# Reordering the DMA queue and VectorE's program of a fused modulated-linear and per-token head-attention kernel

## What is computed

```
def modulated(x, s, aff_w, aff_b, w, b):          # one layer, per batch
    style = s @ aff_w.T + aff_b                   # 512 numbers
    demod = rsqrt(sum((w * style)**2, axis=in) + 1e-8)
    return (x * style) @ w.T * demod + b

x  = x + clip(modulated(x, cond, L0 ...), -256, 256)         # layer L0
kx = modulated(x, cond, K ...).reshape(tokens, 16 heads, 32)  # layer K; q = k = v = kx
A  = softmax(kx @ kx.T / sqrt(32))                # per token, 16 x 16 over its own heads
x  = x + modulated((A @ kx).reshape(tokens, 512), cond, O ...)   # layer O
```

## Time and profile before

| | us |
|---|---|
| three runs: median (lowest to highest) | 783.5 (782.16 to 788.72) |
| the profiled execution, its own time | 782.16 |
| its span, first to last instruction | 780.4 |
| what lies around the span | 1.8 |
| PE busy | 723.8 (93%) |
| PEld (weight loads) busy | 702.9 (90%) |
| VectorE busy | 553.3 (71%) |
| ScalarE busy | 510.1 (65%) |
| transfers of the one hardware queue, share of 16 DMA engines | 78.4% |

### The profile page before, as it was taken

One profiled execution on the slowest core, in us unless ns is written; L12 is line 12 of the kernel. 1 busy time (PEld: TensorE's weight loads), 2 busy tenths in 40 slices (PEclk: granted clock), 3 DMA queues, 4 the chain that ended last, 5 costly groups with the idle time before them and its releaser, 6 DMA issues.

```text
span 780.4 us, 21455 instructions
## 1 busy us (share of the span) xinstructions
PE 723.8 (93%) x8848; PEld 702.9 (90%) x8848; DVE 553.3 (71%) x1040; ACT 510.1 (65%) x1036; POOL 11.7 (1%) x8
## 2 busy tenths in 40 slices
PE   5999788999999999999999999999999999998676
PEld 4999678989999999999999999999999999997566
DVE  4555765778877777787787777778788777776562
ACT  4265547767776766777676677777677776675353
POOL 2300000000000000000000000000000000000000
PEclk9799898999999999999999999999999999998888
DMA  8028686898889988888878988888888889876763
GB/s 297 28 63 198 160 194 185 225 220 218 202 211 227 230 219 230 227 218 209 214 199 216 220 239 223 228 220 223 221 198 210 220 228 232 213 185 151 167 180 108
DMA packets 235778, 157.15 MB, mean 201 GB/s; under 512 B 143265, under 2 KB 225185, under 8 KB 235681
## 3 DMA queue, kind: packets, MB, share of 16 engines
q1 hardware_dynamic: 235680, 155.78, 78.4%
HBM read 71.85 MB, written 67.11 MB: 178 GB/s over the span
## 4 chain that ended last, share of the span: by engine, by line
DMA 37%; PE 28%; SPq 13%; DVE 9%; ACT 9%; issue 4%; DVEq 0%; ACTq 0%
PE lin_ps L388 21%; DMA yr<-y_turned 14%; DMA k_st<-k_turned 12%; DMA k_turned<-kx 8%; SPq L235 7%; SPq L225 4%; DVE k_rhs L676 4%; ACT y_hi L477 3%; ACT kx L468 3%; PE s_ps L426 3%; PE y_ps L444 2%; PE y_ps L411 2%; DVE p_bd L738 1%; DMA v_turned<-k_rhs 1%; SPq L249 1%
## 5 line engine op out<-in xcount | busy, mean ns | idle before, releaser
L388 PE MATMUL lin_ps<-x_hi,w_hi 128*128 128x256 f32 x1024 | 300.6, 294 | 21.5 <-ACT x_hi L477 14.5
L388 PE MATMUL lin_ps<-x_hi,w_lo 128*128 128x256 f32 x1024 | 292.8, 286 | 0.0
L388 PE MATMUL lin_ps<-x_lo,w_hi 128*128 128x256 f32 x1024 | 292.6, 286 | 0.0
L388 PEld LDWEIGHTS lin_ps<-x_hi,w_hi 128*128 128x128 f32 x1024 | 196.9, 192 | 35.1 <-issue 29.3
L388 PEld LDWEIGHTS lin_ps<-x_lo,w_hi 128*128 128x128 f32 x1024 | 197.8, 193 | 0.0
L388 PEld LDWEIGHTS lin_ps<-x_hi,w_lo 128*128 128x128 f32 x1024 | 197.2, 193 | 0.0
L388 PE MATMUL lin_ps<-y_hi,w_hi 128*128 128x256 f32 x512 | 147.6, 288 | 12.0 <-DVE y_lo L626 7.9
L388 PE MATMUL lin_ps<-y_lo,w_hi 128*128 128x256 f32 x512 | 146.7, 287 | 0.0
L388 PE MATMUL lin_ps<-y_hi,w_lo 128*128 128x256 f32 x512 | 146.5, 286 | 0.0
L477 ACT ACTIVATE x_hi<-x,style 128x256 fp32r<-128x256 f32 x256 | 115.1, 499 | 36.9 <-DVE x L697 27.1
L626 DVE SCALAR_TENSOR_TENSOR x_lo<-x,style,x_hi 128x256 fp32r<-128x256 f32 x256 | 109.5, 480 | 10.7 <-ACT x_hi L477 10.6
(11 more groups left out here) (48 smaller groups left out, 667.8 us busy)
## 6 DMA issues: line engine op xcount, KB each, us to landing
x<-xT SPq DMA_DIRECT2D x32, 512.0 KB, 6.0
k_turned<-kx SPq DMA_DIRECT2D x32, 512.0 KB, 3.6
k_st<-k_turned SPq DMA_DIRECT2D x128, 128.0 KB, 4.0
k_bd<-k_rhs SPq DMA_DIRECT2D x128, 128.0 KB, 2.4
v_turned<-k_rhs SPq DMA_DIRECT2D x32, 512.0 KB, 6.6
k_v<-v_turned SPq DMA_DIRECT2D x128, 128.0 KB, 3.7
y_turned<-y SPq DMA_DIRECT2D x128, 128.0 KB, 3.2
yr<-y_turned SPq DMA_DIRECT2D x32, 512.0 KB, 5.0
```

The lines of the kernel that those rows point to most:

```text
L388: mm = pe.matmul(lin_ps[:, n % NLB, 0:T], w[:, k, m * P:(m + 1) * P], r[:, k, :], start=(q == 0), stop=(q == len(passes) - 1))
```

## The change

Two lists are reordered; no instruction is added, removed or resized.

On SP, in each iteration of the loop: `v_from_dram`, which stood second and served tile i-2, now stands last and serves tile i-1, right behind `v_to_dram(i-1)` and the store; `y_from_dram(i-3)` and `load_x(i+2)` now stand ahead of `spread_k(i-1)` instead of behind it. Head and tail of the list follow the same pattern (`k_from_dram` ahead of `v_from_dram`, `spread_k` behind `y_from_dram`), and `store(0, 0, 1)` moves ahead of the loop.

On VectorE, in the loop and the tail: `turn_k(i-1)` moves from between the halves of `make_x1(i)` to behind `x1_lo_of(i, 1)`.

```diff
             k_to_dram(1)
+            k_from_dram(1)
             v_from_dram(0)
-            k_from_dram(1)
             load_x(5)
             spread_k(1)
             v_to_dram(1)
             k_to_dram(2)
+            k_from_dram(2)
             v_from_dram(1)
-            k_from_dram(2)
             spread_k(2)
             v_to_dram(2)
             k_to_dram(3)
+            k_from_dram(3)
             v_from_dram(2)
-            k_from_dram(3)
             y_to_dram(0)
-            spread_k(3)
             y_from_dram(0)
             load_x(6)
+            spread_k(3)
             v_to_dram(3)
             y_to_dram(1)
             y_from_dram(1)
+            v_from_dram(3)
+            store(0, 0, 1)
             for i in range(DEPTH + 1, N):
                 k_to_dram(i - 1)
-                v_from_dram(i - 2)
                 k_from_dram(i - 1)
                 y_to_dram(i - 3)
-                spread_k(i - 1)
                 y_from_dram(i - 3)
                 if i < N - 2:
                     load_x(i + 2)
+                spread_k(i - 1)
                 v_to_dram(i - 1)
-                if i == DEPTH + 1:
-                    store(0, 0, 1)
                 if i < last:
                     store(i - 4, 0, 1)
+                v_from_dram(i - 1)
             k_to_dram(last)
-            v_from_dram(last - 1)
             k_from_dram(last)
             y_to_dram(last - 2)
+            y_from_dram(last - 2)
             spread_k(last)
-            y_from_dram(last - 2)
             v_to_dram(last)
             v_from_dram(last)
...
             def dve_steps(i):
                 c0, c1, c2, c3, c4 = range(i, i - 5, -1)
                 return [
-                    (c2, normalise), (c0, make_x1, 0), (c2, spread_probabilities), (c1, turn_k), (c0, make_x1, 1),
-                    (c0, x1_lo_of, 0), (c0, x1_lo_of, 1), (c4, finish, 0), (c2, turn_v),
+                    (c2, normalise), (c0, make_x1, 0), (c2, spread_probabilities), (c0, make_x1, 1),
+                    (c0, x1_lo_of, 0), (c0, x1_lo_of, 1), (c1, turn_k), (c4, finish, 0), (c2, turn_v),
...
             dve_tail = [
-                (last - 2, normalise), (last, make_x1, 0), (last - 2, spread_probabilities), (last - 1, turn_k),
-                (last, make_x1, 1), (last, x1_lo_of, 0), (last, x1_lo_of, 1), (last - 4, finish, 0),
+                (last - 2, normalise), (last, make_x1, 0), (last - 2, spread_probabilities), (last, make_x1, 1),
+                (last, x1_lo_of, 0), (last, x1_lo_of, 1), (last - 1, turn_k), (last - 4, finish, 0),
```

## The result

| | kernel before | changed kernel |
|---|---|---|
| median of the runs (lowest to highest), us | 782.83 (774.04 to 788.72, 4 runs) | 830.5 (830.08 to 832.03, 4 runs) |
| the profiled execution / its span, us | 782.16 / 780.4 | 827.42 / 825.6 |

The kernel before has a fourth run here, beside the three of its table. The ratio is 1.0652, with a 95% interval of 1.0564 to 1.0741: the change makes the kernel 6.5% slower. The forecast was 795.5 us in a range of 764 to 818: the right sign, about a quarter of the size.

A forecast was written before the change was run, and what follows sets the result against it. Before, TensorE's 21.2 us a tile and the DMA round of k and y were nearly equal bounds. A 22.5 us serial SP round gave 782.2 + 18 (loop) - 4 (head) - 2 (tail) = 794.2, 795.5 by the median; range 764 to 818.

The forecast's parts named there:

- SP's list becomes one serial round: SP's loop: issuing and exposed landings of k, y and v add up in series to 22.5 us a tile, against 21.77.
- step 4: SP's round, from y_from_dram issued to v_to_dram landed: 9.1 us, ends 7.5 and 11.6.
- step 1: SP's round, k_to_dram from issued to landed: 3.7 us, with 3.0 to 5.3 as the ends seen before.
- The likeliest case: The loop: a round of 22.3 to 23.7 us a tile, chance 0.42; own range 22.0 to 23.2, 783 to 813 us.
- The wait that decides: SP at v_from_dram(i-1): waits over 3 us for the v_to_dram just issued, with k_to_dram(i) and the next round behind it.
- `turn_k` in time: VectorE: turn_k ready 7.1 us after k_from_dram's first issue, before SP reaches spread_k at 8.4; moving it gives nothing more.
- the first rival: The loop: SP's round stays under TensorE's 21.2 us a tile, both removed waits are gain, 760 or 761 us; chance 0.28.
- `yr` earlier, K's evacuation earlier: SP and K's evacuation: yr no longer waits for turn_k and spread_k's issuing; k_to_dram could come some 2.5 us earlier.
- No charge for the clock: TensorE: waits of some 1.3 us a tile leave the granted clock at 1.00, so no time was added.
- TensorE as the bound: The loop: SP's round stays under TensorE's 21.2 us a tile, giving 760 or 761 us; chance 0.28.
- Break-even: The loop: round of 21.7 to 22.3 us, the head giving back the loss, time near 782 us; chance 0.20.
- The heavier queue: SP's round: slower k_bd, v_from_dram and k_to_dram make 24.4 us a tile, 843 us; chance 0.10 for rounds over 23.7.

The follow-up runs named there:

- e12: The kernel before with only y_from_dram moved ahead of spread_k and load_x behind v_to_dram; turn_k and v_from_dram in old places: 762.42 us, ratio 0.981.
- e9: e1 with v_from_dram(i-2) moved from second to third place, behind k_from_dram: 795.53 us, ratio 1.024 to the kernel before.
- e1: The changed kernel without the v_from_dram move; y_from_dram and load_x stay ahead of spread_k, turn_k behind x1_lo: 771.02 us, ratio 0.990 to the kernel before.
- e5: The changed kernel with turn_k back in its old place between the halves of make_x1: 832.96 us, ratio 1.074 to the kernel before.
- e7: The changed kernel with load_x moved behind v_to_dram: 801.95 us, ratio 1.033 to the kernel before.
- e11: The changed kernel with v_to_dram moved ahead of spread_k: 801.09 us, ratio 1.031 to the kernel before.
- e10: e1 with one SP wait added at each iteration's end, for v_to_dram(i-1) to land; nothing moved: 775.0 us, ratio 0.999 to the kernel before.
- e3: The kernel before with only turn_k moved behind x1_lo on VectorE: 842.43 us, ratio 1.081.
- e8: e1 with load_x moved behind v_to_dram: 776.26 us, ratio 1.002 to the kernel before.
- e4: The kernel before with only y_from_dram and load_x moved ahead of spread_k: 779.62 us, ratio 0.998.
- e2: The kernel before with only v_from_dram moved to the loop's end, and k_from_dram ahead of it in the head: 822.15 us, ratio 1.054.

## Why the prediction was right or wrong

**The floor and what bounds before: right.** The floor of about 21.2 us a tile was reached in e12 (21.10), whose 25 tiles take 16.7 us less than before; 25 x 0.59 had said 14.8.

**SP's list becomes one serial round: right, and it is the cause.** In the changed kernel SP's only waits for other engines are 27.6 us for `turn_k` and 4.8 for `x1`, and the two-tile chain through TensorE (see e9) has room: `k_to_dram(c+2)` goes out 27.2 us after scores(c) start, where 21.7 to 21.9 are needed in e1 and e9. The sum's terms, as predicted and as 24 tiles (5 to 28, as in all means over 24 tiles here) of the changed kernel show them; their round of 23.8 is 23.66 over the 25 tiles of the loop:

| term | predicted | measured |
|---|---|---|
| 1. `k_to_dram` to landed | 3.7 | 4.2 |
| 2. `k_from_dram`, issuing | 2.0 | 2.0 |
| 3. `y_to_dram` to landed | 5.2 | 4.9 |
| 4. `y_from_dram` issued to `v_to_dram` landed | 9.1 | 10.1 |
| 5. `v_from_dram`, issuing | 2.4 | 2.3 |
| steps between | 0.1 | 0.3 |
| round | 22.5 | 23.8 |

**The term that was mis-sized is step 4, by 1.0 us, and after it step 1, by 0.5.** Against a loop of 21.77 the forecast was a difference of two near numbers, 0.73 us a tile, so 1.2 us more over the 25 tiles makes the loss 2.6 times as large: 47.4 us in place of 18. I had taken the spacing of `x` behind `yr` as 1.9 us and that of `k_bd` as 1.6, from one tile of the head; e5 shows 2.5 and 2.1, and 1.2 for v behind `k_bd`, as assumed. Both 2.5 and 2.1 lie outside the ends I gave for one step. e7 and e11 show the term at work: with 512 KB less ahead of v it is 8.4 and 7.8 us, and the kernel is 3% over before in place of 6.5%.

The 35 us between 795.5 and the measured 830.5 are 29.4 in the loop, 3.9 in head and tail, and 1.8 because the median here lies 3.1 us above the profiled execution, not 1.3. The likeliest case was a round of 22.3 to 23.7 us, and the measured one lies at its very end; the stated time range stopped at 818.

**Step 1** was taken from the median of an order in which `k_v` goes out behind k. With the four `k_v` just ahead, the last of which landed 2.8 us after k's issue, it was 4.2; in e7, where the store too was on its way for another 1.5 us, 5.2.

**"The wait that decides": wrong in its share.** The prediction put the price on the wait for v. e10 has a wait for v at that place, 1.2 us a tile, and costs 0.8% over e1; e9 has the issuing moved without that wait and costs 3.4% over it (1.024 to 0.990), by another chain; wait and issuing in series cost 7.6% (1.065 to 0.990). Neither is the price by itself: what decides is whether the whole list comes out above TensorE's 21.2 us and the slack. The sum had all the pieces, but its words put the weight on one. A run with the full 3.9 us of waiting and the issuing left in its old place was not made.

**`turn_k` in time, its move worth nothing more: right for the time, wrong in detail.** SP did wait for `turn_k`, 27.6 us in 17 waits, where I had computed slack. I had timed `turn_k` by the landing of `k_st` alone, although the edit puts it behind `x1_lo`, and `x1_lo` behind the softmax work when the scores come late; at 423.11 us it starts right behind `x1_lo`. But e5, without that wait, has the same round. What I missed is that the edit is not harmless by itself: alone it costs 8.1% (e3), and with `load_x` late it is the difference between 0.981 (e12) and 1.002 (e8); only where `spread_k` stands behind `load_x` does it seem to give something, from 0.998 (e4) to 0.990 (e1), whose intervals just touch. The gain that the first rival expected, no wait in front of K(i), comes from the earlier `yr` without it: e4 and e12 have it with `turn_k` in its old place.

**`yr` earlier, K's evacuation earlier: right.** In e1, e4 and e12 the wait in front of K(i) went, and ScalarE's wait for `yr`, 60.8 us in 25 waits before (160 to 700 us), fell to 0.6 (e12) and 2.3 (e1).

**No charge for the clock: wrong in the trace, of little weight.** I expected gaps of 1.3 us; in 10 of the 25 tiles PE's were 2.7 to 4.2, and the granted clock over the loop was 0.96. PE was busy 13.6 us longer for it (547.73 against 534.12). e5 has gaps of 2.9 us at most, a granted clock of 0.98 over its loop, and the same round, in which SP hardly waits for another engine, so the slower matmuls lie beside SP's round.

**The signs.** SP's waits for v (3.9 us in each of 23) and y (2.3), none for K's evacuation, and K(i) without a gap came as stated; TensorE waited for `k_bd` 19 times. One sign failed: `v_turned` was to land more than 5 us after its issue, and its median is 4.7, since SP reached `v_to_dram` later than assumed. In e5 it is 6.2.

**Head: wrong, tail: right.** Scores(3) did come 3 us sooner (125.6 against 128.6), but `store(0, 0, 1)` and `v_from_dram(3)` now stand ahead of `k_to_dram(4)`, which landed at 135.3 in place of 133.2; `k_bd(4)` came late and TensorE waited 3.9 us for it. -4 was predicted and +0.7 measured. The tail gave 2.8 us, predicted 2.

**The rivals.** TensorE as the bound: what e12 is, and not the change. Break-even: that is where e10 came out, and not the change. The heavier queue at 24.4 us a tile, to which I gave 0.10 from 23.7 on, was the nearer case: 23.66 lies 1.2 us above the forecast and 0.7 below it. Theory B of the experiments, that `k_bd` behind `yr` and `x` is the cost, falls with e1 (fast with that order) and e2 (slow without it). That `turn_k`'s place is the main cost falls with e5, which leaves it where it was and is as slow. That the page on DMA would come out another way (the Trainium skill, "DMA: Bandwidth & Descriptors", "Anatomy of one DMA — SWDGE (gpsimd) path": 2 us plus bytes at 436 GB/s, an estimate of 6.8 us for step 4) is not borne out for this path: 10.1 us.

**Left open.** Why `k_bd` takes 2.1 us of the queue and v 1.2 for the same bytes wasn't tried apart: `k_bd` moves inside SBUF in four transfers and v goes out in one. The loops of e7 and e11, 22.7 us a tile each, lie between SP's round and the two-tile chain of e9, and I have no closed sum for them. The changed kernel without any DMA wait on SP wasn't tried: taking those waits away would be a race.

## What to carry to other kernels

Where one engine issues all DMAs in a fixed list, add up that list as a round of its own: issuing, each landing waited for in the open, and the depth of the queue ahead of it; in the changed kernel it was the bound, and no busy share showed it. Put other issuing, already released, between a transfer's issue and the wait for it: taking it out of there cost 3.4% in e9. And take landing times from places with the same load in front: a sum that decides by 0.7 us in 22 doesn't survive terms read from a quiet stretch.

## What was not expected of the hardware

Transfers of 512 KB issued on one queue within 4 us landed one behind the other, and the step depended on the kind: 2.5 us for `x` from HBM behind `yr`, 2.1 for the four `k_bd` inside SBUF, 1.2 for v from SBUF to DRAM (24 tiles of e5). Issuing `k_bd` up to 4 us later did not make v land later, as long as `yr` and `x` were still ahead (10.1 us in the changed kernel, where it went out 2.4 us behind `yr` in the mean, against 10.2 in e5, where it was 1.0; single tiles with 3.6 to 4.1 us have 9.5 to 10.3).

The granted clock fell to 0.50 after idle times of TensorE of 1.75 to 2.0 us in six of the seven falls in e3's loop (3.0 us before the seventh). In the loop of the kernel before, the longest idle time of PE was 1.4 us, and the clock stayed at 1.00.
